# The last tile's two products and its add and store, made in two column halves

## The reference, cut to what matters

```
def _L1_ffn_ref(x, W, b, Wq, Wk, A, Bm):
    result = einsum('bsi,oi->bso', x, W) + b                 # "dense"
    q, k   = x @ Wq.T, x @ Wk.T                              # 8 groups of 32
    w      = softmax(einsum('bsed,bsed->bse', q, k) / sqrt(32))
    h      = einsum('bsi,eri->bser', x, A)
    combined = einsum('bse,bser,eor->bso', w, h, Bm)         # "combine"
    return result + combined

x = x + _L1_ffn_ref(_L1_cond_ref(x, ...), ...)               # the output
```

## Time and profile before

| | |
|---|---|
| time, median of 3 runs | 230.16 us (230.13 to 230.21) |
| span of the profiled execution, first to last instruction | 228.5 us |
| TensorE busy | 217.1 us (95%) |
| VectorE busy | 134.6 us (59%) |
| ScalarE busy | 85.0 us (37%) |
| mean granted TensorE clock | 1.000 of full |

### The profile page before, as it was taken

The page is one execution under the profiler, slowest core; times in us unless marked ns, Lnnn a source line. Parts: engine busy times, 40 slices in busy tenths (PEclk is TensorE's granted clock), DMA queues, the critical chain, the costliest instruction groups (busy, mean ns, idle before and its releaser), DMA issues.

```text
span 228.5 us, 3173 instructions
## 1 busy us (share of the span) xinstructions
PE 217.1 (95%) x1181; PEld 186.1 (81%) x1181; DVE 134.6 (59%) x279; ACT 85.0 (37%) x165; POOL 62.0 (27%) x72
## 2 busy tenths in 40 slices
PE   2787999999999999999999999999999999999994
PEld 2777886788788888999888888888998998999982
DVE  4998589876943334957462113445997555435442
ACT  6946576745954441123531013442112211211110
POOL 2504022545146643206300002442262220122000
PEclk9999999999999999999999999999999999999999
DMA  5999944200000000007526000000000110110103
GB/s 141 258 392 390 317 59 68 34 0 0 0 3 0 0 0 0 3 0 116 84 35 75 17 3 1 0 0 0 3 0 0 46 49 0 47 46 3 46 4 135
DMA packets 30400, 13.56 MB, mean 59 GB/s; under 512 B 24936, under 2 KB 25512, under 8 KB 30384
## 3 DMA queue, kind: packets, MB, share of 16 engines
q1 hardware_dynamic: 30288, 13.33, 22.2%
q10 hardware_dynamic: 96, 0.03, 0.1%
HBM read 11.26 MB, written 2.10 MB: 58 GB/s over the span
## 4 chain that ended last, share of the span: by engine, by line
PE 87%; DVE 9%; DMA 1%; ACT 1%; issue 0%
PE PS L1121 25%; PE PS L1122 25%; PE PS L1123 24%; PE PS L1133 7%; DVE XS L437 5%; PE PS L1243 3%; DVE up_lo L798 2%; DMA wc_nat<-in_L_cond_weight_dram 1%; DVE H_lo L920 1%; DVE dn_lo L972 0%; ACT fc_hi L690 0%; PE PS L1147 0%; PE PS L1146 0%; PE PS L1272 0%; PE PS L1359 0%
## 5 line engine op out<-in xcount | busy, mean ns | idle before, releaser
L845 DVE TENSOR_TENSOR PS<-PS,relu 128x512 f32<-128x512 f32 x16 | 11.1, 693 | 32.4 <-ACT relu L624 32.4
L1121 PE MATMUL PS<-H_hi,up_hi 128*128 128x512 f32 (+1 forms) x80 | 28.3, 354 | 0.0
L1122 PE MATMUL PS<-H_lo,up_hi 128*128 128x512 f32 (+1 forms) x80 | 27.9, 349 | 0.0
L1123 PE MATMUL PS<-H_hi,up_lo 128*128 128x512 f32 (+1 forms) x80 | 27.8, 347 | 0.0
L1133 PE MATMUL PS<-wconv,XS 128*128 128x128 f32 x192 | 25.0, 295 | 2.0 <-DVE wconv L913 1.5
L1133 PEld LDWEIGHTS PS<-wconv,XS 128*128 128x128 f32 x192 | 24.3, 210 | 2.5 <-DVE wconv L913 1.6
L1121 PE MATMUL PS<-qkT_hi,H_hi 128*128 128x320 f32 x64 | 20.3, 317 | 0.1
L1122 PE MATMUL PS<-qkT_lo,H_hi 128*128 128x320 f32 x64 | 19.8, 309 | 0.0
L1123 PE MATMUL PS<-qkT_hi,H_lo 128*128 128x320 f32 x64 | 19.8, 309 | 0.0
L624 ACT ACTIVATE relu<-PS 128x512 f32<-128x512 f32 x16 | 9.5, 597 | 25.1 <-PE PS L1123 25.1
L570 POOL TENSOR_TENSOR X<-X,rowb 128x512 f32<-128x512 f32 x8 | 10.3, 1288 | 31.3 <-PE PS L1243 31.3
(11 more groups left out here) (189 smaller groups left out, 476.5 us busy)
## 6 DMA issues: line engine op xcount, KB each, us to landing
up_raw<-in_L_ffn_up_w_dram SPq DMA_DIRECT2D x2, 1024.0 KB, 8.0
dn_raw<-in_L_ffn_down_w_dram SPq DMA_DIRECT2D x2, 1024.0 KB, 12.9
out_dram<-X SPq DMA_DIRECT2D x8, 256.0 KB, 2.0
X<-in_x_dram SPq DMA_DIRECT2D x1, 1024.0 KB, 15.2
XS<-in_L_ffn_W_dram SPq DMA_DIRECT2D x16, 64.0 KB, 2.3
X<-in_x_dram SPq DMA_DIRECT2D x2, 256.0 KB, 3.4
X<-in_x_dram SPq DMA_DIRECT2D x1, 512.0 KB, 5.4
fc<-in_L_ffn_fc_w_dram SPq DMA_DIRECT2D x1, 512.0 KB, 3.6
```

The source lines that it names most:

```text
L845: nc.vector.tensor_tensor(U[i % 2], U[i % 2], relu[:], ALU.mult).then_inc(s_sq, 1)
L1121: nc.tensor.matmul(o, lh, rh, start=start, stop=False)
L1122: nc.tensor.matmul(o, lh, rl, start=False, stop=False)
L1123: return nc.tensor.matmul(o, ll, rh, start=False, stop=stop)
```

## The change

The last tile d is handled in two halves of 256 columns. Half 0 is made in bank `D[3]`, half 1 in bank `D[0]`, which tile a had used. dense(d) and combine(d) become two calls each; combine(c) and turn_hw(d) stand between the dense halves. DVE adds each half when its combine is made, and does finish(c) ahead of hw_split(d). SP stores the first half of tile d, and ACT issues the store of the second.

```diff
+        def last_half(i):
+            return (D[(TILES - 1) % TPH], D[0])[i][:, i * L // 2:(i + 1) * L // 2]
...
@@ sync
                 sp.wait_ge(s_fin, T + 1)
-                sp.dma_start(out_dram[:, T, :], X[:, T, :]).then_inc(s_out, 16)
-            sp.wait_ge(s_out, 16 * TILES)
+                ls = slice(0, L if T < TILES - 1 else L // 2)
+                sp.dma_start(out_dram[:, T, ls], X[:, T, ls]).then_inc(s_out, 16)
+            sp.wait_ge(s_out, 16 * (TILES + 1))
@@ scalar
             hw_split(c)
             hw_split(d)
+            act.wait_ge(s_fin, TILES + 1)
+            act.dma_start(out_dram[:, d, L // 2:L], X[:, d, L // 2:L]).then_inc(s_out, 16)
@@ vector
+            def finish_halves(T):
+                dve.wait_ge(s_x1b, T + 1)
+                for i in range(2):
+                    dve.wait_ge(s_res, T + 1 + i)
+                    ls = slice(i * L // 2, (i + 1) * L // 2)
+                    nc.vector.tensor_tensor(X[:, T, ls], last_half(i), X[:, T, ls], ALU.add).then_inc(s_fin, 1)
...
             finish(b)
+            finish(c)
             hw_split(d)
-            finish(c)
-            finish(d)
+            finish_halves(d)
@@ tensor
+            def dense_half(T, i):
+                ts = slice(T % TPH * P, (T % TPH + 1) * P)
+                ls = slice(i * L // 2, (i + 1) * L // 2)
+                if i:
+                    pe.wait_ge(s_fin, TILES - TPH + 1)
+                for p in range(PH):
+                    mm3(last_half(i), H_hi[:, p, ts], H_lo[:, p, ts], wT_hi[:, p, ls], wT_lo[:, p, ls], p == 0, False)
+
+            def combine_half(T, i):
+                ls = slice(i * L // 2, (i + 1) * L // 2)
+                pe.wait_ge(s_hwT, T + 1)
+                mm3(last_half(i), hwT_hi[:, T % 2], hwT_lo[:, T % 2], bT_hi[:, ls], bT_lo[:, ls], False, True)\
+                    .then_inc(s_res, 1)
...
             combine(b)
-            dense(d)
+            dense_half(d, 0)
+            combine(c)
             turn_hw(d)
-            combine(c)
-            combine(d)
+            dense_half(d, 1)
+            combine_half(d, 0)
+            combine_half(d, 1)
```

## The result

| | before | changed |
|---|---|---|
| median of 12 executions each | 230.20 us (230.03 to 231.92) | 229.54 us (229.16 to 231.17) |
| ratio of the means | | 0.9949, 95% interval 0.9926 to 0.9972 |
| span of the profiled execution | 228.5 us | 227.9 us |

The kernel became faster. The median is 0.66 us lower, where 0.72 was forecast (229.44). Its interval reaches to 0.9972, so the forecast ratio, 229.44 / 230.16 = 0.9969, is still inside. So there are two questions: whether the tail did what the steps said, and where the rest of the ratio comes from.

A forecast was written before the change was run, and what follows sets the result against it. PE was taken to bound the kernel, with its tail wait and 3.17 us after its last matmul exposed. Earlier add end 0.42 plus shorter landing 0.30 gave 0.72 off 230.16: 229.44 us, range 229.2 to 230.05.

The forecast's parts named there:

- Steps 1 and 2: PE's tail: 30 half-width matmuls cost 0.09 us more; turn_hw(d) moves ahead of the second dense half, last start 224.90.
- step 1: PE's dense(d) and combine(d): 256-column matmuls 0.120 us apart, +0.09 us in all, dense(d) starting at 220.59 in both kernels.
- Step 3: PE's wait ahead of combine(d) for DVE's hw split, 0.27 us, is hidden with 0.42 us to spare.
- Step 4: DVE's last add in two halves of 0.42 us each, the second ending at 225.64 against 226.06.
- Steps 5 and 6: Tile d's stores: half the bytes land in 1.7 us, not 2.0; nothing added for ACT's queue.
- The rival of packets that cost by their number: Tile d's half stores don't shrink: gain 0.12 us if they queue, 0.42 if not; chance 0.18.
- ACT's queue: Rival at the last store: long-idle queue lands in 2.6 us, a loss of 0.17, time 230.33; chance 0.10.
- The sum: Whole tail: 0.42 us from the earlier add end plus 0.30 from shorter landing, 0.72; 230.16 becomes 229.44 us.
- How the numbers follow: Whole kernel: about 0.2% (0.46 us) is measurable; faster 0.68, same 0.27, slower 0.05; range 229.2 to 230.05.
- theory A: Follow-up expectation, whole kernel: change worth 0.6 us; long executions equally likely for both, by chance more on the kernel before.

The follow-up runs named there:

- e7: The kernel before with 12 matmuls without a use in PE's standstill between 16.7 and 18.6 us; 230.69 us, ratio 0.9996.
- e8: The kernel before with only its tail order changed, no column halves, plus 12 matmuls without a use in PE's standstill; 230.41 us, ratio 0.999.
- e10: The kernel before with 6 matmuls without a use in PE's standstill ahead of 18.6 us; 230.21 us, ratio 0.9976.
- e11: The changed kernel with tile d stored whole, plus 6 matmuls without a use in PE's standstill; 229.80 us, ratio 0.9948.
- e3: The changed kernel with tile d stored whole by SP after the second add; 229.80 us at full clock, ratio 0.9995.
- e2: The changed kernel with SP, not ACT, issuing the second half's store too; 229.63 us at full clock, ratio 0.9981.
- e5: The changed kernel unchanged, third time, against the kernel before; 229.56 us at full clock, ratio 0.9983.
- e14: The changed kernel unchanged, fourth time, against the kernel before; 229.54 us at full clock, ratio 0.9985.
- e9: The changed kernel with 6 matmuls without a use in PE's standstill ahead of 18.6 us; 229.59 us, ratio 0.9942.
- e13: The changed kernel with 6 matmuls without a use in PE's standstill, run a second time; 229.54 us, ratio 0.9938.
- e6: The changed kernel with 12 matmuls without a use in PE's standstill between 16.7 and 18.6 us; 230.01 us, ratio 0.9961.

## Why the prediction was right in its steps and wrong in its range

**Steps 1 and 2, the matmuls.** 256-column matmuls cost 0.117, not 0.120: the 30 cost 0.01 more than the 15, not 0.09. The second behind the transpose came after 0.20, not 0.22. PE's last start was 224.85, forecast 224.90, although dense(d) began 0.04 later than step 1 took for granted.

**Step 3, the wait.** Right. DVE's split ran at 223.55 (forecast 223.53). Counted as the prediction counts it, PE could go 0.35 behind that, at 223.90, and came at 224.26: 0.36 to spare where 0.42 was forecast. PE did not wait. By itself the removed wait is worth 0.28 us (e7 against e8), forecast 0.27.

**Step 4, the adds.** The end was right, 225.65 for 225.64, with some luck: the first half's last matmul started 0.04 earlier than forecast (224.50), DVE followed it by 0.39 and not 0.32, and the two adds took 0.76 and not 0.78. What the column halves bring without their store is the rest of the 0.65: 0.65 - 0.28 - 0.24 (the split store, below) = 0.13. Run against run says the same: e10 less e11 is 230.21 - 229.80 = 0.41, of which 0.28 is the order.

**Steps 5 and 6, the stores.** The half landed in 1.7 (SP) and 1.8 (ACT), forecast 1.7; the last one is ACT's, so here the sum was 0.1 too high. e3 and e11 against the changed kernel give 0.28 and 0.21 for the split store, forecast 0.30. The rival of packets that cost by their number fell: both halves moved within some 0.85 us, where it had 0.67 for each. The Trainium skill's sentence on disjoint halves (DMA: Bandwidth & Descriptors, Rules for kernel authors) is about partition halves, and these were halves of the columns; in e2's windows they too went one behind the other. What was gained is that the first half could be issued before the second add was done. The prediction said that no row shows two stores in flight together. The earlier trace rows do show it: tile c's store, issued at 225.13, lands at 227.1, and tile d's is issued at 226.09. Only their data did not move at the same time. ACT's queue was not slow after 220 us of rest (1.8); e2, with SP for both, was 0.1 slower at full clock.

**The sum.** Over all comparisons the changed kernel's median at full clock is 229.52 us (31 executions), that of the kernel before 230.17 (71): 0.65 us, 0.28%, where 0.72 was forecast. The profile's 0.6 agrees; the 0.1 of ACT's landing is the greater part of what is missing.

**What failed** is the section "How the numbers follow": its first sentence, that a measurement of this kernel can tell about 0.2% (0.46 us) from no change, and the sum's one time for the kernel before. They put at nothing, without a reason, that TensorE's clock differs from one execution to the next. The range was built from the unknown costs of the tail around one time for the kernel before, 230.16 us. That kernel has two times, 230.17 and 231.76; the profile and the three executions that I had were all of the first kind. Over all comparisons it showed the second in 69 of 140 executions, the changed kernel in 17 of 48. In the first comparison the shares were 5 of 12 and 1 of 12: means of 230.76 and 229.65, ratio 0.9952. Of the 1.11 us between these means 0.65 are the change; four executions more in the longer group are worth 4 / 12 x 1.6 = 0.53 us, which covers the rest (the sum of 1.18 is 0.07 too high, as the five long ones here were a little shorter than most). In e5 and e14 the same kernel, with 6 and 8 of 12, got 0.9983 and 0.9985. So the 0.5% of the first comparison was luck of the draw: theory A, chance, is what these runs fit best. The trace before shows PE's waits at the start but a clock of 1.00 behind them, so it could not have told of the second time; only more executions of the kernel before would have, or a range widened for what three of them cannot show.

**Shown and not shown.** That the 1.6 us come from half the clock between 19.7 and 23 us is shown by e2's windows, for one execution. That it does not happen without the standstill of 1.9 us ahead is shown by filling it: 0 of 95 executions had 0.993 (the one of 365.77 us is not counted), against 105 of 224 in all unfilled kernels. Whether the earlier waits have a part in it was not tested. Why it happens in one execution and not in the next is open; so is whether the changed kernel has it a little more rarely (17 of 48 against 69 of 140, but 1 to 8 of 12 from run to run).

**A version that beats both** is e9 and e13: the changed kernel with the filler of 6. The median of its executions but the one named is 229.54, and its ratios to the kernel before are 0.9942 (0.992 to 0.9964) and 0.9938 (0.9913 to 0.9963). It gains over the changed kernel by the clock alone: in the comparison that held both, the mean was 229.51 (e13) against 230.60 (e14), at the same 229.54 at full clock.

## What to carry to other kernels

Where the last result waits on a chain through three engines, put independent matmuls between the chain's start and its use; here that order, without any halving, gave 0.28 us. Halving the last add and store gives less than half of each, since most of a store's 2.0 us does not shrink (1.7 to 1.8 for half the bytes), and a part of 192 columns bought nearly nothing from PE over one of 256 (0.111 against 0.117 us). Before a change of 0.3% is judged by a ratio, look at the clock of each execution: here what followed a standstill of PE early in the program added 1.6 us to half of them, more than twice what the change is worth, and six matmuls without a use took that away.

## What was not expected of the hardware

A PE standstill of 1.9 us was followed, about 1.2 us after PE had resumed (18.33 to 19.5 in e2), by some 3.3 us at the lower clock in nearly half of the executions; 1.4 us of filling in it were enough to prevent that. The Trainium skill (TensorE: Matmul & The Clock Gate, HAM oscillation) names waits of TensorE as what lets its clock fall. The runs agree that it is the wait, for filling it kept the clock up in 95 of 95; this one is shorter than the waits of that section's example. The filler's float32 matmuls, written once, were carried out as two instructions each (12 in the source of e6, 24 in the trace). These start 0.111 us apart; the 0.118 in what was expected of e9 is 2.84 / 24, which counts the last one's full length. Matmuls of 128 and of 192 columns started at the same distance of 0.111 us, those of 256 at 0.117 in the tail and 0.120 at the start.
